# An attention and spline layer in hand-ordered instruction streams: masks, weight splits, stores and row loads change places

## The reference

```
x = x + xattn(layernorm(x), ctx, seg_id, W...);  x = x + ffn(layernorm(x), ...)
xattn:  kv_c = kv @ W_kvc;  q_c = q @ W_dq
        q_nope = q_c @ W_uq;  q_rope = rope(q_c @ W_qr)
        k_nope = kv_c @ W_uk;  v = kv_c @ W_uv;  k_rope = rope(kv_c @ W_kr)
        scores = (q_nope . k_nope + q_rope . k_rope) * scale
        good = (k_ids <= seg_id) & (k_ids >= seg_id - 8);  scores = where(good, scores, NEG)
        out = softmax(scores) @ v;  return out @ W_o
ffn:    normalise, pick one of 64 tiles per row by sign scores, look up a 16-point spline, scale, add
```

## Time and profile before

| | |
|---|---|
| median of 3 runs | 3094.92 us (3091.76 to 3104.9) |
| profiled execution, its time | 3093.33 us |
| its span | 3091.5 us |
| mean granted TensorE clock | 0.976 |
| PE busy | 2931.5 us, 95% of the span |
| DVE, ACT, POOL busy | 2173.5 us (70%), 1642.4 us (53%), 944.4 us (31%) |
| chain that ended last | PE 71%, DVE 6%, ACT 3% |
| DMA | mean 192 GB/s |

### The profile page before, as it was taken

One profiled execution on the slowest core, in us unless ns is written; L12 is line 12 of the kernel. 1 busy time (PEld: TensorE's weight loads), 2 busy tenths in 40 slices (PEclk: granted clock), 3 DMA queues, 4 the chain that ended last, 5 costly groups with the idle time before them and its releaser, 6 DMA issues.

```text
span 3091.5 us, 41471 instructions
## 1 busy us (share of the span) xinstructions
PE 2931.5 (95%) x13886; PEld 2376.3 (77%) x13886; DVE 2173.5 (70%) x4546; ACT 1642.4 (53%) x3220; POOL 944.4 (31%) x685
## 2 busy tenths in 40 slices
PE   8999868999999999999999999999999999999985
PEld 6777757888778878888788887788788887888862
DVE  4555645777677775777767776777757777677776
ACT  3655634655365563655446553655636554455553
POOL 6265562211412214222232114122142222321127
PEclk9999999999999999999999999999999999999985
DMA  7564646555665546555665556655475556655431
GB/s 252 194 207 177 216 179 241 175 180 179 241 214 187 183 165 258 188 188 183 228 234 175 180 179 242 213 191 176 166 262 188 188 183 228 218 171 181 146 110 5
DMA packets 178304, 592.74 MB, mean 192 GB/s; under 512 B 38304, under 2 KB 52256, under 8 KB 141744
## 3 DMA queue, kind: packets, MB, share of 16 engines
q1 hardware_dynamic: 173024, 589.21, 54.8%
q0 software_dynamic: 5072, 0.88, 0.7%
HBM read 471.31 MB, written 85.14 MB: 180 GB/s over the span
## 4 chain that ended last, share of the span: by engine, by line
PE 71%; DVE 6%; ACT 3%; issue 2%; DMA 1%; POOL 1%; ACTq 0%; SPq 0%; DVEq 0%; POOLq 0%
PE psD L2605 9%; PE psA L2528 7%; PE psC L2623 7%; PE psB L2537 5%; PE psE L2623 5%; PE psT L2592 5%; PE psD L2548 3%; PE psS L2564 3%; PE psA L2480 3%; PE psS L2565 3%; PE psS L2577 3%; PE psS L2573 3%; PE psS L2574 3%; PE psB L2480 2%; PE psA L2519 2%
## 5 line engine op out<-in xcount | busy, mean ns | idle before, releaser
L1474 ACT ACTIVATE exps_ring<-exps_ring,neg_max 128x512 f32<-128x512 f32 x512 | 370.7, 724 | 396.2 <-DVE neg_max L1904 395.3
L1488 ACT ACTIVATE probsT_hi<-psT 128x512 fp32r<-128x512 f32 x432 | 258.2, 598 | 412.5 <-PE psT L2592 408.5
L1904 DVE CUSTOM_DVE_ANT_0 exps_ring<-psS,mask 128x512 f32<-128x512 f32 x512 | 352.3, 688 | 167.1 <-PE psS L2577 146.5
L1916 DVE TENSOR_TENSOR probsT_lo<-psT,probsT_hi 128x512 fp32r<-128x512 f32 x432 | 297.5, 689 | 181.9 <-ACT probsT_hi L1488 181.5
L1480 ACT ACTIVATE exps_ring<-exps_ring,row_sum_inverse 128x512 f32<-128x512 f32 x512 | 368.7, 720 | 44.9 <-DVE row_sum_inverse L1910 44.8
L2623 PE MATMUL psC<-w_o_product,attn_product 128*128 128x512 f32 x1302 | 355.4, 409 | 22.2 <-POOL w_o_product L1109 11.5
L2623 PEld LDWEIGHTS psC<-w_o_product,attn_product 128*128 128x128 f32 x1302 | 236.1, 192 | 72.9 <-issue 16.0
L2623 PE MATMUL psE<-w_o_product,attn_product 128*128 128x512 f32 x1008 | 272.3, 405 | 0.0
L2592 PE MATMUL psT<-ident,exps_ring 128*128 128x128 f32 x1728 | 261.3, 274 | 10.9 <-DVE probsT_lo L1916 10.9
L2592 PEld LDWEIGHTS psT<-ident,exps_ring 128*128 128x128 f32 x1728 | 209.2, 140 | 77.9 <-issue 27.5
L2528 PE MATMUL psA<-q_c_hi,w_uq_ring 128*128 128x512 f32 x768 | 262.9, 397 | 1.2 <-POOL w_uq_ring L1141 1.1
(11 more groups left out here) (488 smaller groups left out, 6554.0 us busy)
## 6 DMA issues: line engine op xcount, KB each, us to landing
w_o_product<-w_o_split SPq DMA_DIRECT2D x190, 1024.0 KB, 5.3
w_uq_ring<-w_uq_split SPq DMA_DIRECT2D x112, 384.0 KB, 4.7
w_o_split<-w_o_product SPq DMA_DIRECT2D x28, 1024.0 KB, 5.5
w_uk_ring<-w_uk_split SPq DMA_DIRECT2D x112, 256.0 KB, 2.9
w_uv_quad<-w_uv_split SPq DMA_DIRECT2D x28, 1024.0 KB, 6.9
w_qr_sorted<-w_qr_split SPq DMA_DIRECT2D x28, 768.0 KB, 4.2
x_stage<-in_x_dram SPq DMA_DIRECT2D x32, 512.0 KB, 5.3
x_stage<-in_ctx_dram SPq DMA_DIRECT2D x32, 512.0 KB, 5.8
```

The lines of the kernel that those rows point to most:

```text
L1474: act.activation(E[:, qt, :], E[:, qt, :], ACT.Exp, scale=-1.0, bias=mx[:, i % 2, qt:qt + 1], accum_out=rs[:, i % 2, qt:qt + 1]).then_inc( ...
L1904: dve.tensor_tensor_reduce(E[:, qt, :], psS[qt % 2][:, :], mask[:, qt, :], -SCALE, BIG, ALU.add, ALU.min, mx[:, i % 2, qt:qt + 1]).then_in ...
L1916: dve.tensor_tensor(PT[1][:, :, qt * P:(qt + 1) * P], turn_bank(q, i, qt)[:, :].rearrange("p (c n) -> p c n", c=TT), hi.bitcast(F32), ALU. ...
```

## The change

Only orders change, and with them who does the last two weight subtractions. **SyncE**, batch 0: the writing and loading of the next quad's rotary weights go behind `split_after(q, 3)`; `put_o(q-1, 6)` and the raw load behind it (`room_w_next`) go behind the 16 stack transfers. In the passage from batch 0, `w_dq_lo` goes behind `put_o(3, 1)`, and ctx rows 6 and 7 ahead of `put_o(3, 4)`; in the others `load_o(3, 2)` goes between `w_dq_hi` and `w_dq_lo`. The stores of x1 tiles 0 and 2 go behind the first head's stack. **GpSimd**, batch 0: `split_quad` interleaves weight splits, sums and `w_o` differently, and at its end the masks of batch 1 come behind the last weight sum, `wo_sum(3, 4)`. **VectorE** takes `wo_lo(3, 5)` and `wo_lo(3, 6)` (`last_wo_lo`), makes `product_lo(b, 0, 0)` sooner, and reorders the passages. **ScalarE**: `uk_hi`, `qr_hi`, `uv_hi` go behind `expo(3)`; `attended` behind `q_hi`, `k_hi`; `product_hi(b, 0, 0)` ahead of `expo(2)`; `wo_hi(q, 0)` sooner. **TensorE** turns x tile 3 ahead of `product(3, 1, 1)` in every passage.

```diff
@@ SyncE: order in batch 0
-                else:
+                split_after(q, 3, n + 2, None if end else (nxt, 1))
+                if not end:
                     put_qr(nxt, q + 2)
                     if nxt + 1 < NQ:
                         raw_qr(nxt + 1, qr_raw)
-                split_after(q, 3, n + 2, None if end else (nxt, 1))
...
                     if end:
                         load_xs(1, 2)
+                        room_w_next(q)
                     else:
                         raw_o_first(q)
-                    put_o(q - 1, 6)
-                    raw_o_w(q)
...
                         into(b, q, (q + 1) % NQ)
+                        if q > 1:
+                            room_w_next(q - 1)
@@ SyncE: the passage
                     load_dq(b + 1)
                     if first:
                         weights(1)
-                    weights(2)
-                    if not first:
+                        load_dq_lo(b + 1)
+                        load_xs(b + 1, 5)
+                        weights(2)
+                        load_kvc(b + 1)
                         weights(3)
-                    load_xs(b + 1, 5)
-                    load_kvc(b + 1)
-                    if first:
+                        load_xs(b + 1, 6)
+                        load_xs(b + 1, 7)
+                        weights(4)
+                    else:
+                        weights(2)
+                        load_dq_lo(b + 1)
                         weights(3)
-                    weights(4)
-                    load_xs(b + 1, 6)
-                    load_xs(b + 1, 7)
+                        load_xs(b + 1, 5)
+                        load_kvc(b + 1)
+                        weights(4)
+                        load_xs(b + 1, 6)
+                        load_xs(b + 1, 7)
...
-                    into(b + 1, 0, 1, odd_tiles)
+                    into(b + 1, 0, 1, even_tiles, odd_tiles)
@@ GpSimd: split_quad, batch 0
+                uq_lo(q, 2, uq_raw)
                 if not q0:
+                    sum_of_quad(0, q - 1, 1)
+                    sum_of_quad(0, q - 1, 2)
                     wo_lo(q - 1, 1)
                     wo_sum(q - 1, 1)
-                uq_lo(q, 2, uq_raw)
                 uk_lo(q, 2, uk_raw)
                 if not q0:
-                    late_sums(0, q - 1)
+                    sum_of_quad(0, q - 1, 3)
                     wo_lo(q - 1, 2)
-                    wo_sum(q - 1, 2)
+                uq_lo(q, 3, uq_raw)
@@ GpSimd: end of batch 0 (all of it new order)
+                    rstds(1, [2])
                     wo_lo(NQ - 1, 0)
+                    load_seg(1)
+                    wo_lo(NQ - 1, 1)
+                    rstds(1, [3])
+                    wo_sum(NQ - 1, 1)
+                    sum_of_quad(0, NQ - 1, 1)
+                    sum_of_quad(0, NQ - 1, 2)
+                    wo_lo(NQ - 1, 2)
+                    c = mask_begin(1)
+                    sum_of_quad(0, NQ - 1, 3)
+                    wo_sum(NQ - 1, 2)
+                    wo_lo(NQ - 1, 3)
+                    wo_sum(NQ - 1, 3)
+                    wo_lo(NQ - 1, 4)
+                    wo_sum(NQ - 1, 4)
+                    mask_tile(c, 1, 0)
+                    rope_lo(1, 0)
+                    for t in range(1, TT):
+                        mask_tile(c, 1, t)
@@ ScalarE: a head
                     if late:
                         q_hi(b, *following)
                         k_hi(b, *following)
+                        if i == HQ - 1:
+                            product_hi(b, q, 0)
                     expo(b, q, i, 2)
...
-                    if i > 0 and not late:
+                    if i > 0 and plain_quad(b, q):
                         attended(b, *before)
...
-                    if first and ahead[0] < NQ:
-                        uk_hi(*ahead, n_ahead, uk_raw, (q, i))
...
                     if following is not None and not late:
                         q_hi(b, *following)
                         k_hi(b, *following)
-                    if first and q > 0 and i < HQ - 1:
+                    if i > 0 and not late and not plain_quad(b, q):
+                        attended(b, *before)
+                    if first and i == HQ - 1:
+                        wo_hi(q, 0)
+                    elif first and q > 0:
                         wo_hi(q - 1, (1, 3, 5)[i])
@@ VectorE
+            def last_wo_lo(j):
+                n = prod_no(0, NQ - 1, j)
+                dve.wait_ge(s_woh, n + 1)
+                dve.tensor_tensor(WO[:, n % 2, 1], wo_source(NQ - 1, j),
+                                  WO[:, n % 2, 0].bitcast(F32), ALU.subtract).then_inc(s_wo[n % 2], 16)
...
+                    if late and i == HQ - 1:
+                        product_lo(b, q, 0)
                     piece(2)
+                    if not late:
+                        turned_lo(b, q, i, 0)
                     if at_end:
                         norm_stats(b + 1, 2)
-                    if not late:
-                        turned_lo(b, q, i, 0)
...
+                    if at_end:
+                        norm_x(b + 1, 2)
-                    if i == HQ - 1 and not plain_quad(b, q):
+                    if i == HQ - 1 and q > 0 and not plain_quad(b, q):
                         product_lo(b, q, 0)
@@ TensorE: the passage
                 product(b, o, 1, 0)
+                turn_stage(b + 1, 3, False)
                 product(b, o, 1, 1)
-                turn_stage(b + 1, 3, False)
```

112 lines of the change are left out of this document (53 added, 59 removed).

## The result

| | before | changed |
|---|---|---|
| median | 3095.09 us (4 runs, 3091.76 to 3104.9) | 3053.47 us (4 runs, 3053.14 to 3053.89) |
| profiled span | 3091.5 us | 3051.7 us |
| mean granted TensorE clock | 0.976 | 0.979 |
| PE, DVE busy | 2931.5, 2173.5 us | 2927.9, 2187.4 us |
| ACT, POOL busy | 1642.4, 944.4 us | 1640.2, 943.6 us |

The ratio of the times is 0.986, with a 95% interval of 0.9838 to 0.9883: the kernel became 41.6 us faster. The forecast was 3040 us with a range from 3025 to 3062. So the result lies in the range, 13.5 us above the forecast.

What follows compares the result with a forecast made beforehand. The prediction took TensorE to bound the kernel wherever it is fed, so reordering returns only waits and half-clock time. Passage 34, every batch 13 and batch 0 7 make 54 us off 3093.33: 3039.3, stated as 3040, range 3025 to 3062.

Steps and rivals of the forecast that it cites:

- The passage, 34 us: Passage from batch 0 to 1: loads of ctx rows no longer late, first score near 467.5 us; bounds 29 to 36 us.
- the first rival: Passage from batch 0: the masks become the bound, one late operand stops TensorE after two tiles; 3046 us, chance 0.12.
- VectorE's two low parts at no cost: Passage from batch 0: two weight subtractions moved to VectorE, 1.8 us each, cost nothing because VectorE idles or has slack.
- Every batch, 13 us: Waits that return in every batch: 9.8 + 3.3 + 2.0 - 2.1 = 13.0 us gained, bounds 5 and 16.5.
- The 3.3 us for `q_lo`: Every batch: `q_hi` 0.6 us sooner covers twenty of the 21 waits of 0.17 us for `q_lo`; 3.3 us gained.
- The charge for the passages: Six passages: `turned_lo` ahead of `norm_stats` delays VectorE, 0.35 us each, 2.1 us lost.
- Batch 0, 7 us: Batch 0: fewer waits for `q_lo` and `w_o_product` and less half-clock time, less boundary losses; bounds 0 and 16 us.
- the price of the boundaries: Three quad boundaries of batch 0: `wo_lo(q-1, 0)` later behind `uk_lo(q, 1)`, 0.4 to 0.7 us each; 1.8 us lost.
- The clock, 3 us: Batch 0: stretches at the lower clock behind short waits within quads shrink; 3 us gained of 12.8 at most.
- The second: Batch 0 gives nothing: waits for `q_lo` return as waits for `w_o_product`; 3047 us, chance 0.13.
- The third: Another transfer, `w_dq_lo` or ctx rows 6 and 7, is 10 to 15 us late; 3050 to 3055 us, chance 0.10.
- The fifth: Slower: `attended` behind `q_hi` and `k_hi`, 1.2 to 1.9 us later, 72 times; 3125 to 3170 us, chance 0.03.

Runs made afterwards that it cites:

- the second measurement: The changed kernel once more with no edit, against the kernel before: 3059.66 us (5 runs) against 3090.71, ratio 0.9901.

## Why the prediction was right or wrong

**The passage, 34 us: right.** It gave 32.6. The rows were issued at 435.80 (near 433 in the text), the first score came at 469.35 (467.5), the masks end 2.9 us behind its start ("within 2 us"). Of the chain that the prediction drew from the earlier trace rows, masks ahead of a low part, a store behind it, rows behind the store, two links were put back one at a time: 15.6 us for the masks and 2.8 for the rows. The margin of 1 us for the masks was too good. The low part for product 4 started at 436.71 and not at 433.3, the block from there to the last mask took 35.6 us and not 34.3, and so the masks ended 4.7 us after the 467.6 of the sum and the first score came 1.9 us after its 467.5; the 1.5 us taken off for lateness nearly cover that. The wait for VectorE's first masking was 2.07 us, below the 3 that would have made the first rival; TensorE lost 0.5 us by it, in the quad behind.

**VectorE's two low parts at no cost: right**, and underrated. The prediction gave them a price of nothing, and nothing is what they cost TensorE. Its 1.8 us for one, taken as the time of the subtraction by itself, was a reading at fault: the earlier trace rows already had GpSimd's mask steps beside them. It gave them no gain of their own either; left on GpSimd they would have taken back 24.3 of the 32.6 us.

**Every batch, 13 us: 5.9 measured.** Of its terms, 9.8 for `product_hi` was right in kind and size (8.9 by the run with it put back, for 10.6 us of waits). The 3.3 us for `q_lo` was the step that failed: "`q_hi` comes 0.6 us sooner, which covers twenty of the 21 waits". It did cover them, but the run with them put back shows that they carried no time: what it covered came back as gaps of under 0.15 us elsewhere. The charge for the passages, 0.35 us each, was right in sign and too small: they lengthened by 0.4 each, and by more if two other things are set apart. The waits ahead of the first score, 0.2 to 0.8 us in four of the six passages before, are gone: 2.1 us, near the 2.0 that the prediction gave to the stacks. And one passage of each kernel had 3.4 us at the lower clock (88.04 us before, 87.26 changed). The passages without either took 85.43 and 85.49 us before, and 86.24 to 86.34 in the changed kernel where no wait for `w_dq_lo` adds to them: 0.8 more each. The prediction's cause was `turned_lo` ahead of `norm_stats`. The profile does have six `probsT_lo` waits of 1.39 us, and the passages of 85.76 and 85.79 us in the run with the old order speak for some 0.5 of the 0.8. What the prediction did not charge is `load_o(3, 2)` ahead of `w_dq_lo`, a transfer of 1 MB in front of one of 1.5 MB. It had priced `w_dq_lo` behind a transfer only in the passage from batch 0. With `w_dq_lo` ahead of it the six passages fall to 516.02 us, 3.6 less than in the changed kernel and 7.6 less than in the run beside it, and each takes 85.90 to 86.09 us, some 0.3 less than the 86.24 to 86.34 above.

**Batch 0, 7 us: 1.9 measured, and the largest miss against what was possible.** The 5.9 us for `q_lo` and `w_o_product` within quads seem to have come, in quad 1 alone: 7.4, though that code took from 88.4 to 92.5 us for the quad in seven traces. The step that failed is the price of the boundaries: "some 0.4 to 0.7 us later each", "1.8 us lost". The stretches from quad 2 on lengthened by 5.7 us. Of the three waits for `w_o_product` that were to be longer, the one near 135 us fell from 4.19 to 2.90; the two near 227 and 318 rose from nothing and 0.74 to 2.94 and 2.48, by three to five times the price of a boundary. I had looked at one cause, `uk_hi` late on ScalarE, and not at what SyncE's queue does there: the raw rows of `w_o` are issued behind a store that waits 17.1 us. The prediction had moved each piece on its own engine and did not ask when the operand of `wo_sum` lands. The runs show that place: the loads sooner give 8.4 us, and with the low part sooner as well 15.4. The seven traces of that code lie between 248.2 and 253.0 us for the three, the one trace of the kernel before at 249.9, so the 1.9 us itself is within what varies, and the gain of batch 0 may as well be none; the 15.4 is not within it.

**The clock, 3 us: nothing.** "The stretches behind short waits within quads should shrink." Before and after, 27.3 us from 130 to 449 us ran at the lower level; one of the new ones, 223.07 to 229.90, begins in the middle of the boundary waits shown above. In the runs that leave those boundaries as they are it was 20.5 to 41.0 us; with the raw rows sooner it fell to 10.2, and with the low part sooner as well to 6.8.

**The rivals.** The second, batch 0 gives nothing, is what happened in the main, by its own words: waits for `q_lo` came back under another name, and the waits for `w_o_product` in batch 0 were 11.2 us, just short of its mark of 12. Its price was 3047. The remaining 6 us are those of the later batches. The third, another transfer late, happened with `w_dq_lo`, at about a tenth of the size that I gave it for each passage. The fifth, `attended` as the new bound, did not happen: the run with `attended` first is the same within 2 us. (Its upper price was added up wrong: 3039 and 137 us are 3176, not 3170.)

**The sum.** The range was met by its largest term. The whole gain was forecast as 54 us and measured as 41.6, and as 31 in the second measurement; by that one it is little more than half of the forecast, while its time, 3059.66 us, still lies in the range.

## What to carry to other kernels

A block of work with a late due time, here 29 us of masks, belongs behind every short operation whose result goes through a store or another engine; ask for each operation in a block what transfer it releases, and what that transfer is queued ahead of. When an order is changed on several engines at once, follow the operand of each moved instruction back to the issue of its load: a queue of transfers in written order passes on every wait, and 8 us lay in a load issued behind a store that was not needed yet, 7 more in a low part that stood behind others on GpSimd. And sum no small waits that occur once in every head: put them back by themselves first, since 4.1 us of waits carried no time at all, and 10.6 us of others carried 8.9.

## What the runs showed of the hardware that was not expected

- A load of 1.5 MB landed 10.7 to 11.1 us after its issue (medians of seven) behind one other load of its size, and 12.2 us with a third transfer between the two, of 1 MB in six of the seven. The 1 to 1.5 us are enough to stop TensorE in two or three passages of six.
- VectorE's addition of 128x512 with both operands in SBUF took 0.69 us with GpSimd idle and 1.10 to 1.14 us when it started 0.1 us behind a GpSimd mask step. It ended before that step did (806.20 and 806.54), so it was slowed and not held until the step's end.
- The same program's stretches with many transfers differ from run to run: 88.4 to 92.5 us in quad 1 of batch 0 (seven traces), 518.9 to 523.6 over the six later passages. Its 18 unsplit quads stay within 1303.3 and 1303.8.
